# Random features: VectorE adds the eighth weighted value block onto the first in twelve of sixteen tiles, and the constant shift becomes a ninth half square

## The reference, cut to what matters

```python
p = jnp.einsum('...d,ed->...e', x, R)            # 8 angles a head
feats = jnp.concatenate([jnp.sin(p), jnp.cos(p)], axis=-1) / math.sqrt(F)
kv  = jnp.einsum('bhsf,bhsd->bsfd', kp, v)       # summed over heads, token by token
out = jnp.einsum('bhsf,bsfd->bhsd', qp, kv)
```

## Time and profile before

| | us |
|---|---|
| median of 3 runs (1091.32 to 1095.9) | 1095.19 |
| the profiled execution | 1095.49 |
| its span in the trace | 1093.8 |
| PE busy / PEld busy | 1013.9 / 830.2 |
| DVE busy | 715.5 |
| ACT busy / POOL busy | 464.3 / 394.9 |
| `gather` (L2681), 256 rows on PE | 59.2 |
| `weigh` (L2908), `total` (L2894), `shift` (L2900), 16 each on DVE | 36.5, 19.3, 5.4 |
| `differences` (L2590), 16 on POOL | 65.6 |

### The profile page before, as it was taken

One profiled execution on the slowest core, in us unless ns is written; L12 is line 12 of the kernel. 1 busy time (PEld: TensorE's weight loads), 2 busy tenths in 40 slices (PEclk: granted clock), 3 DMA queues, 4 the chain that ended last, 5 costly groups with the idle time before them and its releaser, 6 DMA issues. The chain is left out here.

```text
span 1093.8 us, 18248 instructions
## 1 busy us (share of the span) xinstructions
PE 1013.9 (93%) x6343; PEld 830.2 (76%) x6343; DVE 715.5 (65%) x1725; ACT 464.3 (42%) x797; POOL 394.9 (36%) x475
## 2 busy tenths in 40 slices
PE   7799995799999999988999989999899998899997
PEld 4688884665565665577788978888788986888886
DVE  4954445997888877465544457765669887656554
ACT  6533341356666655543433412323365534232222
POOL 4446654445554621205676400000126647100000
PEclk9899998988999988888999989999999899999999
DMA  7624426000000032134642150000010300000000
GB/s 235 211 74 155 145 70 203 2 1 2 3 1 22 2 117 88 40 130 176 215 143 92 64 198 1 1 1 1 1 77 1 78 1 1 1 1 21 20 20 20
DMA packets 39180, 71.97 MB, mean 66 GB/s; under 512 B 10610, under 2 KB 28082, under 8 KB 38836
## 3 DMA queue, kind: packets, MB, share of 16 engines
q1 hardware_dynamic: 29492, 48.25, 13.4%
q0 software_dynamic: 7488, 20.46, 5.6%
q10 hardware_dynamic: 2112, 2.10, 0.6%
HBM read 46.78 MB, written 23.87 MB: 65 GB/s over the span
## 5 line engine op out<-in xcount | busy, mean ns | idle before, releaser
L2341 PE MATMUL ps<-xt,w 128*128 128x512 f32 x768 | 192.1, 400 | 4.1 <-PEq L439 2.7
L2341 PEld LDWEIGHTS ps<-xt,w 128*128 128x128 f32 x768 | 142.0, 191 | 34.5 <-DVE xt L212 4.5
L2021 DVE CUSTOM_DVE_ANT_0 ps<-ps,att_mask 128x128 f32<-128x128 f32 (+3 forms) x256 | 119.1, 516 | 29.0 <-PE ps L1579 28.6
L2394 ACT ACTIVATE had_sig<-ps 128x512 f32<-128x512 f32 x64 | 38.3, 599 | 185.9 <-PE ps L2341 185.9
L2435 DVE TENSOR_TENSOR had_gated<-ps,had_sig 128x512 f32<-128x512 f32 x64 | 44.2, 691 | 109.7 <-ACT had_sig L2394 109.7
L1882 ACT ACTIVATE att_early_probs<-ps 128x384 f32<-128x384 f32 (+1 forms) x192 | 91.2, 528 | 51.2 <-PE ps L1594 50.5
L709 POOL DMA_INDIRECT moe_xs<-xn_rows,moe_index x78 | 85.6, 1097 | 59.7 <-DVE moe_index L1207 30.9
L860 PE MATMUL ps<-moe_w,moe_narrow_xb 128*128 x378 | 106.1, 394 | 0.0
L715 POOL DMA_INDIRECT made_rows<-moe_units_made,moe_index x78 | 77.5, 994 | 72.4 <-ACT moe_units_made L1024 60.2
L2355 PE MATMUL ps<-w,had_yhi 128*128 128x256 f32 x512 | 94.4, 282 | 1.8 <-DVE had_ylo L2447 1.8
L1470 POOL TENSOR_SCALAR_AFFINE_SELECT att_early_probs<-att_early_probs 128x256 f32<-128x256 f32 x128 | 54.3, 438 | 113.4 <-ACT att_early_probs L1882 113.1
(11 more groups left out here) (325 smaller groups left out, 2286.1 us busy)
## 6 DMA issues: line engine op xcount, KB each, us to landing
moe_w<-in_moe SPq DMA_DIRECT2D x12, 768.0 KB, 6.9
back<-made_rows SPq DMA_DIRECT2D x14, 512.0 KB, 6.7
x<-x_turned SPq DMA_DIRECT2D x8, 512.0 KB, 8.3
low_weights<-moe_w SPq DMA_DIRECT2D x4, 768.0 KB, 3.6
w_early<-in_moe SPq DMA_DIRECT2D x4, 768.0 KB, 4.4
w_early<-low_weights SPq DMA_DIRECT2D x4, 768.0 KB, 10.9
x<-in_x SPq DMA_DIRECT2D x4, 512.0 KB, 6.2
xn_rows<-moe_wide_xn SPq DMA_DIRECT2D x4, 512.0 KB, 3.6
```

Source lines behind the costliest of these rows:

```text
L2021: last = nc.vector.tensor_tensor_reduce(g.ps[:, a, col:col + n], g.ps[:, a, col:col + n], mask[:, SEQ - n:SEQ], -1.0, 3.0e38, ALU.add, ALU ...
L2341: last = nc.tensor.matmul(g.ps[:, bank(n, half), :], w[a][:, k, c * P:(c + 1) * P], xt[low][:, b % 2, k, :], start=(k == 0 and q == 0), st ...
```

## The change

Four edits. `shift` is gone: `apart` gets a ninth element behind each eight, set once to -0.5 x 8 = -4 at the stage's start (one VectorE memset of 128x384 over the three buffers), and `total` sums nine elements. ScalarE's and GpSimd's instructions work on the first eight of each nine, at the same element count. In the tiles t < 12, VectorE adds block 8 of `wv_prod` onto block 1 (`fold`, 128x256, both inputs in SBUF, waiting for `weigh`), and it is `fold` that then releases `gather`. `gather` has seven matmuls in these tiles and eight in the last four.

```diff
+    folded = lambda t: 1 if t < 3 * BT else 0
+    NINTH = HALF + 1
-        apart = sb("apart", [P, 3, HKV, H, HALF])
+        apart = sb("apart", [P, 3, HKV, H, NINTH])
...
-                    apart[:, t % 3, :, :, :],
+                    apart[:, t % 3, :, :, 0:HALF],
...
-                for k in range(HKV):
+                for k in range(HKV - folded(t)):
...
-                                            start=(k == 0), stop=(k == HKV - 1))
+                                            start=(k == 0), stop=(k == HKV - folded(t) - 1))
...
-                flat = apart[:, t % 3, :, :, :].rearrange("p k h e -> p (k h e)")
+                flat = apart[:, t % 3, :, :, 0:HALF].rearrange("p k h e -> p (k h) e")
                 nc.scalar.activation(flat, flat, ACT.Sin, scale=0.5 * TWO_PI).then_inc(sin_done, 1)
...
-            def shift(t):
+            def weigh(t):
                 dve.wait_ge(summed, t + 1)
-                flat = sums[:, t % 2, :, :].rearrange("p k h -> p (k h)")
-                nc.vector.scalar_tensor_tensor(out=flat, in0=f32(g.ones[:, 0:1]).to_broadcast([P, HKV * H]),
-                                               scalar=-HALF / 2.0, in1=flat, op0=ALU.mult, op1=ALU.add).then_inc(shifted, 1)
-
-            def weigh(t):
-                dve.wait_ge(shifted, t + 1)
...
-                    v[:, t % 8, :, :].unsqueeze(2).to_broadcast([P, HKV, H, HD]), ALU.mult).then_inc(prod_done, 1)
-
+                    v[:, t % 8, :, :].unsqueeze(2).to_broadcast([P, HKV, H, HD]), ALU.mult) \
+                    .then_inc(weighed if folded(t) else prod_done, 1)
+
+            def fold(t):
+                dve.wait_ge(weighed, t + 1)
+                head_of = lambda k: wv_prod[:, t % 2, k, :, :].rearrange("p h d -> p (h d)")
+                nc.vector.tensor_tensor(head_of(0), head_of(0), head_of(HKV - 1), ALU.add).then_inc(prod_done, 1)
+
+            nc.vector.memset(apart[:, :, :, :, HALF:NINTH].rearrange("p s k h e -> p (s k h) e"), -HALF / 2.0)
...
-                if is_tile(s):
-                    shift(s)
                 if is_tile(s + 2):
                     rests(s + 2)
                 if is_tile(s):
                     weigh(s)
+                    if folded(s):
+                        fold(s)
```

More of the change, by code:

```diff
@@ L2547, in features_stage @@
         apart_done, sin_done, sin2_done = sem("apart_done"), sem("sin_done"), sem("sin2_done")
-        summed, shifted, prod_done, ctx_ps, ctx_out = sem("summed"), sem("shifted"), sem("prod_done"), sem("ctx_ps"), sem("ctx_out")
+        weighed = sem("weighed")
+        summed, prod_done, ctx_ps, ctx_out = sem("summed"), sem("prod_done"), sem("ctx_ps"), sem("ctx_out")
         x_stored, x_turned, x_biased, x_added = sem("x_stored"), sem("x_turned"), sem("x_biased"), sem("x_added")
```

## The result

The changed kernel takes 1117.52 us (median of 4 runs, 1114.06 to 1118.02), the kernel before 1095.55 (4 runs, 1091.32 to 1097.08): a ratio of 1.0191, 95% interval 1.0154 to 1.0228, slower by 1.5 to 2.3%. The forecast was 1114.7 us in a range of 1104 to 1123. The profiled execution took 1114.06 us, its span is 1112.3, 18.5 more than before.

The account below looks back on a forecast made before the run. VectorE and TensorE were taken as about equally loaded for two thirds of the features stage, VectorE setting the time after. 29.9 + 0.6 - 3.8 - 0.3 - 7.2 = +19.2 us on 1095.49 gave 1114.7 us, range 1104 to 1123.

Parts of the forecast that it names:

- The fold's price: VectorE behind `weigh`: each of twelve folds waits for GpSimd's `differences` and ends 2.49 us after `weigh`, +29.9 us.
- `wholes` unblocked: VectorE behind folded tiles: five `wholes` no longer wait for GpSimd, 1.11 to 0.35 us each, -3.8 us.
- The ninth square in place of `shift`: VectorE: `total` costs 0.14 us more a tile, dropping `shift` gives back only 0.09; together +0.6 us.
- Net 0.05 x 13: VectorE: longer `total` less what dropping `shift` gives back, over 13 tiles, +0.65 us, taken as +0.6.
- The tail: Tiles 14 and 15: without `shift`, `weigh(14)` meets GpSimd and ends at about 919.2 instead of 919.43, -0.3 us.
- The waits given back: VectorE's waits for TensorE's norms and ScalarE, 818 to 914.7 us, close entirely: -7.2 us, bounds 0 and 7.2.
- The memset: Features stage start: 384 elements set before VectorE's first instruction, which waits 2.38 us for ScalarE; priced at nothing.
- The sum: Whole kernel: 29.9 + 0.6 - 3.8 - 0.3 - 7.2 = +19.2 us, giving 1114.7 us, 1.8% slower.
- (a): Rival: the fold goes ahead of GpSimd, 0.45 us each, mostly paid by waits; -1.5 us, 1094.0 us; chance 0.10.
- (b): Rival: TensorE is the bound throughout the folded tiles, VectorE's waits cover the fold; 1091.5 us; chance 0.02.
- (c): Rival: TensorE's clock stays low from waiting at gathers, six steps of 8.8 us add 11 us; 1126 us; chance 0.08.
- The signs: Expected trace: folds of 2.4 to 2.5 us, VectorE gapless from 818 us, TensorE waiting over 2 us at most gathers.

Follow-up runs that it names:

- e3: Kernel before plus the fold as a one-input tensor_reduce over two blocks, seven matmuls, `shift` kept: 1095.42 us, ratio 0.9989.
- e2: Kernel before plus the fold alone, as a two-input addition into its own tile, seven matmuls, `shift` kept: 1114.93 us against 1097.0.
- e7: Changed kernel with `rests(s+2)` moved behind `weigh(s)` and `fold(s)`, so `differences` is released after the fold: 1099.84 us against 1096.88.
- e6: Changed kernel with a second addition of the same size right behind each fold: 1121.67 us against 1096.88.
- e8: Changed kernel with each fold made by one tensor_reduce, written into free context slots: 1095.65 us against 1096.88, ratio 0.9999.
- e1: Changed kernel with no tile folded and eight matmuls in every gather, leaving the ninth half square alone: 1096.15 us against 1097.0.
- e5: Changed kernel with the folds kept but eight matmuls in every gather: 1115.72 us against 1096.88.
- e9: Changed kernel without the folds, still seven matmuls in the gathers of twelve tiles: 1094.79 us against 1097.15, ratio 0.9967.
- e4: Changed kernel with each fold moved to the next step, behind `angles` and `total`: 1104.34 us against 1097.0, ratio 1.0069.
- e10: Changed kernel with the fold one step later, and ahead of `guess` in steps that begin with it: 1102.85 us against 1097.15.
- e11: As e10, but tiles 3 and 7 keep eight blocks and are released by `weigh`: 1097.61 us against 1098.29, ratio 0.9995.

## Why the prediction was right, step by step

**The fold's price** was the step that carried the sum, and it held: 2.49 us forecast, 2.446 to 2.491 measured, and 917.20 - 912.50 = 4.70 us from `weigh` to the instruction behind the fold, where before 914.67 - 912.47 = 2.20 lay between `weigh` and `total`: 2.50 us a fold. That it is GpSimd, and who goes first, is shown three ways: with one SBUF input the addition isn't held up (e3 against e2), with the release of `differences` behind it neither of the two is (e7), and a second addition in its wake takes 0.41 us (e6). The rule from the Trainium skill, SBUF — State Buffer, section Who interferes with whom, named in the prediction, is borne out here: with GpSimd released during `weigh` the fold took 2.46 us, released behind the fold 0.425. The same section of the Trainium skill says that on trn2 a `tensor_reduce` never contends with GpSimd: the 24 reductions of e3 and e8 agree, at 0.69 to 0.71 us beside `differences`.

**`wholes` unblocked**, -3.8 us: five instances fell from 1.11 to 0.34 us, 5 x 0.77, and the one in step 13 to 0.99. With the folds this is 29.9 - 3.8 = 26.1 forecast; between e1 and the change VectorE's busy time grew by 117.05 - 91.20 = 25.9.

**The ninth square in place of `shift`**, +0.6: mis-sized. `total` grew by 0.13 us, near the 0.14 forecast, and 0.65 us lie between the starts of `wholes` and `weigh` (918.73 to 919.38), as forecast. The step that failed is "Net 0.05 x 13": it let `total` grow and left `wholes` at 1.11. A `wholes` that waits for GpSimd's end starts later and waits less, 0.99 us. In e1 the late steps are 905.80 - 900.77 = 5.03 us from `weigh` to `weigh`, where it was 902.27 - 897.16 = 5.11 before. It came to -1.1 us of busy time in e1, tail included.

**The tail**, -0.3: from `weigh(13)` to `weigh(15)` 8.45 us before (912.47 to 920.92), after it 939.39 - 931.28 = 8.11. In VectorE's timeline `weigh(14)` meets GpSimd as forecast:

```profile
931.28 2.28 DVE L2905 TENSOR_TENSOR fea_wv_prod<-fea_sums,fea_v 128x2048 f32<-128x2048 f32 x1
...
934.86 3.07 DVE L2905 TENSOR_TENSOR fea_wv_prod<-fea_sums,fea_v 128x2048 f32<-128x2048 f32 x1
...
939.39 2.29 DVE L2905 TENSOR_TENSOR fea_wv_prod<-fea_sums,fea_v 128x2048 f32<-128x2048 f32 x1
```

**The waits given back**, -7.2: all four named waits closed. The rest of the window, which also holds gaps that no wait names, fell by 6.3.

**The memset**, hidden at nothing: it took 0.38 us, and VectorE still waited 1.65 us for ScalarE behind it.

**The sum**: +19.2 forecast, +18.5 in the stage. It came this near partly by luck: VectorE's busy time was forecast 1.6 us too high (26.4 against 24.8) and what the waits give back 0.9 too high (7.2 against 6.3), and the two cancel in part. The upper end of the forecast's own range stands in it as 1122 and as 1123 us; its terms give 1122.7 with the tail. In the medians the change measured 22.0 us more, and its own profiled execution was the fastest of its four. Against the 17.9 us of e2 and the 18.8 of e5 this is within the intervals; why the other three executions of the change took 3 us longer than the profiled one isn't settled, since they left no trace.

**The rivals.** (a), the fold going first, is excluded by twelve folds of 2.46 us. In e7, where the fold does go first, the time was 1.0026 of the kernel before, not (a)'s 1.5 us under it: its waits gave back 3.7 us of the 7.2 that (a) counts on (in e7 `rests` comes later too, so this isn't (a) alone). (b), TensorE as the bound, is excluded by e5. (c): the clock did fall, to a mean of 0.85 over the window where it was 0.92 before, and 14 rows took 6.14 us, near the 6.2 of (c), but VectorE, full all the while, set the time. My step in (c) that didn't hold is that TensorE would fall behind VectorE once its gathers are slow: they were, in places, but the six pairs of angle matmuls behind the gather at 874.51 came about 0.22 us apart and not 0.43, and the angles were early enough. Two of them, in TensorE's timeline:

```profile
880.88 0.39 PE L2650 MATMUL ps<-rand_blocks,fea_parts_part_c 128*128 128x64 f32 x2
881.10 0.39 PE L2651 MATMUL ps<-rand_blocks,fea_parts_part_s 128*128 128x64 f32 x2
```

**The signs**: one did not come. TensorE was to wait over 2 us at most gathers of tiles 1 to 11; it did so at four of the eleven.

**What the prediction had not asked** is whether the fold could have paid at all. By e9 against e1 the shorter gathers are worth some 2.7 us at the best, and by e3 and e8 a fold that avoids the wait ends at no change. None of the versions run here that compute the reference's result is measurably faster than the kernel before.

## What to carry to other kernels

Price an added VectorE instruction by what GpSimd is doing at that moment: if it reads two SBUF inputs and a GpSimd instruction that reads SBUF was released ahead of it, as `differences` was here, expect it to cost the rest of that instruction too, here 2.46 us for 0.42 us of work. Before writing another operation, look for another order or another form (a reduction over two strided blocks is an addition with one input). And measure first, by leaving the work out, what the saving on the other engine is worth: here it was under 0.3%, and the cheapest fold that was run used it up.

## What the runs showed that I had not expected

- A late release can cost more on a queue's other work than the instruction itself. With eight of the folds at about 0.4 us and none over 1.07, the kernel still lost 0.7% (e4). Much of that is that the gathers of tiles 3 and 7 stand ahead of a next group's norms in TensorE's queue: with the fold ahead of `guess`, leaving out their two folds brought the ratio from 1.0057 to 0.9995 (e10, e11).
- Who waits behind whom can be chosen at little cost: in e7 GpSimd's busy time in the window fell from 63.96 to 36.45 us only because `rests` moved behind two VectorE instructions.
- A reduction of 512 elements with the two blocks strided took 0.69 us, and in none of its 24 instances (e3, e8) more than 0.72, beside a `differences` that kept its usual 4.34 us.
